# A twelve-phase decoder kernel: tree routing of all batches first, tile steps woven into the dense query chunks, five slot and sixteen weight buffers, and exponentials in halves

## The chip, the core and the metric

The kernel runs on one core of a Trainium2 chip. The core has TensorE (PE, matrix products and transposes), VectorE (DVE), ScalarE (ACT), GpSimd (POOL) and SyncE (SP). Each engine runs its own list of instructions in order, and they wait for each other through semaphores. The metric is the device time of one launch in microseconds, the lower the better. Tensors have 128 partitions; a matrix product writes PSUM banks of 512 float32 a partition.

## What is computed

x has 64 sequences of 64 tokens with 128 features. Twelve residual blocks run one after the other, each on the layer norm of x. Two kinds matter here. The first is softmax attention with 8 or 16 heads, in five of the blocks. The second is the third block, a memory attention whose queries, keys and values each come from a hard tree of experts:

```python
def _fff(x, node_w, node_b, w1, b1, w2, b2):
    cur = jnp.zeros((N,), jnp.int32)
    for _ in range(DEPTH):                      # DEPTH = 4: 15 nodes, 16 leaves
        pw = node_w[cur]
        score = jnp.einsum('nd,nd->n', xf, pw) + node_b[cur]
        cur = 2 * cur + 1 + (score >= 0).astype(jnp.int32)
    leaf = cur - N_NODES
    sel = jax.nn.one_hot(leaf, N_LEAVES, dtype=xf.dtype)
    hidden_all = jax.nn.relu(jnp.einsum('nd,ldh->lnh', xf, w1) + b1[:, None, :])
    hidden = hidden_all * sel.T[:, :, None]     # leaf width 64
    out = jnp.einsum('lnh,lho->no', hidden, w2) + sel @ b2

q, k, v = _fff(x, q_...), _fff(x, k_...), _fff(x, v_...)
x = x + softmax(q @ k.T / sqrt(128)) @ v        # inside each sequence of 64 tokens
```

## The kernel before

decoder() runs twelve phases with a barrier between them. x stays on chip. Phase 2 is trees(); phases 0, 3, 7, 9 and 10 are attention().

**trees().** The 4096 tokens are 32 tiles (NT), or 8 groups (g) of 512, or 4 batches (b) of 1024 for the routing. The names P = 128, GT = 4, NG = 8, NC = 8 run through it.

Routing of a batch: norm and shift_mean on DVE and root on POOL give the layer norm's factors. normalize on ACT writes xn. turn_x and take_x transpose it, score_nodes (PE) multiplies with the 45 nodes of the three trees, and decide, levels and count (DVE) make one-hot leaves and counts. turn_leaves (PE) and take_leaves (ACT) transpose the query leaves into selT; negate makes selneg of it. place (PE) and take_places (DVE) give each token its place among those of its leaf. After the fourth batch lay_tiles and give_slots turn places into slots, so that tokens of one leaf fill whole tiles of 128 rows. POOL scatters xn by slot into DRAM, once for the keys (r = 0) and once for the values (r = 1), 32 indirect DMAs each.

The queries are computed densely: for each group and each of 8 chunks of two leaves (m = 0..63), make_hidden(m + 1) multiplies, adds -1e30 to what the token's leaf doesn't hold, relu (ACT) follows, and add_leaf(m) adds up. A group ends with take_q. The order on PE is written out by hand: in front are batches 0 and 1, and batches 2 and 3 are routed inside the chunk loop, with turn_leaves and place at m = 4, 10 and 16.

Keys and values are computed by slot: each region r has 47 tiles (NTL) in 12 steps (NQ) of four. A step m is turn_rows (PE transposes four slots tiles), take_rows (DVE copy), hide_rows (PE), relu_rows (ACT), yield_rows (PE), take_results (DVE) and store_rows (SP). SP loads slots (load_slots, buffers RXS = 3) and a weight block for each tile (load_weights, RW_ = 12 buffers), each weight load behind a read of its row number from table. Steps of r = 0 are woven into the chunks from m = 48 (K_FROM), those of r = 1 run behind the last chunk, with the attention's first pieces between them.

The attention of a group: POOL gathers keys (got_k) and values (got_v, all eight groups in a row, after the last store), turn_k, score, shift, exps, turn_weights, take_weights, weigh (weights times values) and update (x += ...). weigh and update of all eight groups stand behind everything else. PSUM banks are H (two), Y, PJ, SC, XT, HS, YS.

**attention().** 32 tiles i of two sequences each. On PE, in this order: score(i + 1), turn(i), weigh(i), with projections of coming groups between. DVE takes the maximum and subtracts it (shift); ACT takes one exponential of 128x1024 (exps, line 689); turn(i) waits for it and transposes it in two halves of four products into TP, ACT copies each half to pT (take_turned), and weigh(i) multiplies with the values.

## Time and profile before

| | us |
|---|---|
| median of three runs | 2553.05 |
| the runs | 2552.4, 2553.05, 2559.71 |
| the profiled execution | 2557.27 |
| its span in the trace | 2555.3 |
| in it: trees(), from its first to its last instruction | 406.1 to 819.0 |
| in it: TensorE busy | 1864.2 (73%) |
| in it: VectorE, ScalarE, GpSimd busy | 1314.5, 1093.2, 745.8 |

All times in the trace count from the span's start. In its rows stands first when an instruction or a merged run of like instructions begins, then how long it lasts; in brackets how long its engine was idle before it, and which instruction or DMA ended that. SPq is SyncE's issuing of a DMA. Granted clock 1.00 is 2.4 GHz of TensorE and 0.50 is 1.2 GHz.

### The profile page before, as it was taken

How to read it: one execution, taken by the hardware profiler on the slowest of the kernel's cores; microseconds unless marked ns; L12 is line 12 of the kernel's file. 1: busy time of each engine (PE TensorE's matmuls, PEld its weight loads, DVE VectorE, ACT ScalarE, POOL GpSimd, SP SyncE). 2: the span in 40 equal slices, each digit the busy share in tenths (PEclk: the TensorE clock that was granted, in tenths of full speed). 3: DMA queues.
4: the chain of work that ended last, by engine and by line, in shares of the span. 5: the costliest groups of instructions: out<-in, count | busy, mean ns of one | idle time of the engine just before them, and what ended most of it. 6: DMA issues, size and time to landing. Idle time of an engine off the chain costs nothing. (4 is left out here: it accounts for less than half of the span.)

```text
span 2555.3 us, 39295 instructions
## 1 busy us (share of the span) xinstructions
PE 1864.2 (73%) x14689; PEld 1299.7 (51%) x14689; DVE 1314.5 (51%) x3517; ACT 1093.2 (43%) x2105; POOL 745.8 (29%) x625
## 2 busy tenths in 40 slices
PE   3876305897764897978999485997788868862895
PEld 1544203334453465766798353665545535552674
DVE  3887595201122675454343363775278847761223
ACT  3664402332221675843344243773346536630331
POOL 1232101272225321116455001321212122227353
PEclk9888756899655898877999586998879869965897
DMA  4111320024442500001476200000000000001224
GB/s 147 82 82 83 87 79 4 1 82 116 126 108 67 202 2 19 17 13 50 130 235 198 68 1 13 14 10 9 3 1 2 1 13 14 10 23 57 67 79 135
DMA packets 140655, 156.38 MB, mean 61 GB/s; under 512 B 19889, under 2 KB 126065, under 8 KB 139537
## 3 DMA queue, kind: packets, MB, share of 16 engines
q1 hardware_dynamic: 126644, 122.79, 15.5%
q0 software_dynamic: 13248, 28.21, 3.3%
q10 hardware_dynamic: 576, 2.88, 0.3%
q8 instruction: 118, 1.93, 0.3%
q14 instruction: 69, 0.57, 0.1%
HBM read 120.54 MB, written 68.57 MB: 74 GB/s over the span
## 5 line engine op out<-in xcount | busy, mean ns | idle before, releaser
L2696 POOL DMA_INDIRECT f_back<-f_ys,f_row x158 | 151.2, 957 | 177.8 <-DVE f_ys L2857 148.6
L836 PE MATMUL a_AV<-a_vx,a_pT 128*64 128x18 f32 (+1 forms) x3072 | 115.1, 223 | 48.9 <-DVE a_att L529 31.6
L836 PEld LDWEIGHTS a_AV<-a_vx,a_pT 128*64 128x64 f32 x3072 | 105.8, 146 | 79.3 <-issue 32.3
L2689 POOL DMA_INDIRECT f_slots<-f_pay,f_slot x128 | 124.2, 971 | 66.0 <-issue 38.2
L536 DVE TENSOR_REDUCE a_mx<-a_S 128x16 f32<-128x1024 f32 x96 | 117.5, 1224 | 41.0 <-PE a_S L812 39.0
L823 PE MATMUL a_TP<-ident,a_e 128*128 128x128 f32 x768 | 112.6, 295 | 32.7 <-ACT a_e L689 32.2
L823 PEld LDWEIGHTS a_TP<-ident,a_e 128*128 128x128 f32 x768 | 95.9, 152 | 65.6 <-ACT a_e L689 55.4
L689 ACT ACTIVATE a_e<-a_e 128x1024 f32<-128x1024 f32 x96 | 101.3, 1055 | 65.4 <-DVE a_e L539 65.4
L694 ACT COPY a_pT<-a_TP 128x512 f32<-128x512 f32 x192 | 104.1, 589 | 58.2 <-PE a_TP L823 58.0
L812 PE MATMUL a_S<-a_kbd,a_qT 64*64 64x512 f32 x768 | 118.0, 691 | 0.1
L539 DVE TENSOR_TENSOR a_e<-a_S,a_mx 128x1024 f32<-128x1024 f32 x96 | 117.1, 1219 | 1.9
L536 DVE TENSOR_REDUCE x_mx<-x_S 128x16 f32<-128x1024 f32 x64 | 78.4, 1225 | 51.7 <-PE x_S L812 51.2
L2923 ACT ACTIVATE f_h<-f_H,f_wt 128x256 f32<-128x256 f32 x156 | 67.0, 474 | 81.9 <-PE f_H L3019 81.9
L1465 DVE COPY f_xsT<-f_XT 128x512 f32<-128x512 f32 (+1 forms) x24 | 16.3, 681 | 157.3 <-PE f_XT L1697 157.3
L2923 ACT ACTIVATE f_h<-f_H,f_b 128x512 f32<-128x512 f32 (+1 forms) x96 | 58.0, 616 | 83.9 <-PE f_H L3019 83.9
L836 PE MATMUL x_AV<-x_vx,x_pT 128*64 128x18 f32 x2048 | 75.4, 217 | 20.8 <-DVE x_att L529 13.6
L836 PEld LDWEIGHTS x_AV<-x_vx,x_pT 128*64 128x64 f32 x2048 | 69.4, 144 | 40.6 <-issue 23.4
L386 POOL TENSOR_TENSOR x_kbd<-x_kT,x_mask 128x2048 f32<-128x2048 f32 x16 | 57.6, 3600 | 101.9 <-ACT x_kT L666 101.9
L694 ACT COPY x_pT<-x_TP 128x512 f32<-128x512 f32 x128 | 69.2, 589 | 40.1 <-PE x_TP L823 40.1
L674 ACT ACTIVATE a_kbd<-a_kT,a_mask 128x512 f32<-128x512 f32 x128 | 85.6, 723 | 0.4
L823 PE MATMUL x_TP<-ident,x_e 128*128 128x128 f32 x512 | 73.5, 290 | 15.9 <-ACT x_e L689 15.5
L386 POOL TENSOR_TENSOR a_kbd<-a_kT,a_mask 128x2048 f32<-128x2048 f32 x16 | 57.6, 3600 | 90.2 <-ACT a_kT L666 90.2
(478 smaller groups left out, 4724.4 us busy)
## 6 DMA issues: line engine op xcount, KB each, us to landing
f_wt<-in_f_ew SPq DMA_DIRECT2D x39, 584.0 KB
f_slots<-in_blank SPq DMA_DIRECT2D x1, 18576.0 KB
f_wt<-in_f_leaf SPq DMA_DIRECT2D x94, 98.0 KB, 2.0
f_pay<-f_back SPq DMA_DIRECT2D x8, 1024.0 KB, 8.2
f_xs<-f_slots SPq DMA_DIRECT2D x47, 144.0 KB
f_slots<-in_blank SPq DMA_DIRECT2D x1, 5760.0 KB
f_xs<-leaf_slots SPq DMA_DIRECT2D x22, 256.0 KB, 3.0
leaf_out<-f_ys SPq DMA_DIRECT2D x22, 256.0 KB, 2.2
```

Of the source, the lines that this page charges most:

```text
L386: pool.tensor_tensor(kbd[:, n % 2, :, 0:4, :], bc(kT[:, :].rearrange("p (b j) -> p b j", j=SL), 2, shape), mask8[:, 0:4].unsqueeze(1).unsq ...
L536: return v.tensor_reduce(mx[:, i % 2, :], unit(i), AX.X, ALU.max)
L539: v.tensor_tensor(e[:, i % 2, :, :], unit(i), bc(mx[:, i % 2, :], 2, [P, NH, SL]), ALU.subtract).then_inc(shifted.sem, 1)
L674: last = act.activation(kbd[:, n % 2, :, h, :], kT[:, :].rearrange("p (b j) -> p b j", j=SL), ACT.Copy, scale=mask8[:, h:h + 1])
L689: act.activation(e[:, i % 2, :, :], e[:, i % 2, :, :], ACT.Exp).then_inc(weights.sem, 1)
L694: act.copy(pT[:, 4 * n:4 * n + 4, :], TP[:, n, :].rearrange("p (a b) -> p a b", a=4)).then_inc(pT_half.sem, 1)
L812: last = pe.matmul(S[64 * c:64 * c + 64, i % 2, r, :], qT[rows, g % 2, SL * b:SL * b + SL], kbd[rows, g % 2, b, :, :], start=True, stop=True)
L823: last = pe.transpose(TP[:, half, P * n:P * n + P], ev[:, 4 * half + n, :], k.ident[:, :])
L836: last = pe.matmul(AV[64 * c:64 * c + 64, 2 * hp * W1:2 * (hp + 1) * W1], pT[:, hp, 64 * c:64 * c + 64], vx[:, g % 2, t, c, 2 * hp:2 * hp ...
L2689: pool.indirect_dma_start(out=slots[:, :], out_offset=bass.IndirectOffsetOnAxis(ap=slot[:, c, t:t + 1], axis=0), in_=pay[:, c, t, :], in_o ...
L2696: pool.indirect_dma_start(out=back[:, :], out_offset=bass.IndirectOffsetOnAxis(ap=row[:, i % RR, t:t + 1], axis=0), in_=ys[:, i % RY, t, : ...
L2923: act.activation(h[:, i % 2, c, 0:P * n], hid(i, c, n), ACT.Gelu_apprx_tanh, bias=weights(i)[2][:, c:c + 1])\
```

## The change

In trees(): all four batches are routed before the first chunk. On PE place(b - 1) comes behind score_nodes(b), and only turn_leaves(0) stays in front; the other three stand at chunks 8, 14 and 20. negate moves from POOL to DVE. All 24 tile steps stand in the chunk loop, from chunk 23 on (step i = m - 23). Key transposes, scores, weight transposes and value products of the eight groups follow at steps that four tables set (keys_at, scores_at, weights_at, values_at), in and behind the last chunks. Slots get five buffers and weights sixteen, and SP loads them five and four steps ahead of the step whose results it stores. Weights are transposed into HS instead of Y, and the value products go to XT and YS instead of PJ and XT. In attention() the exponential of a tile is two instructions of 128x512, and each half of turn(i) waits for its own.

```diff
@@ attention()
-    scores, shifted, weights = ph.counter("scores"), ph.counter("shifted"), ph.counter("weights")
+    scores, shifted, weights = ph.counter("scores"), ph.counter("shifted"), ph.counter("weights", 2)
...
-                act.activation(e[:, i % 2, :, :], e[:, i % 2, :, :], ACT.Exp).then_inc(weights.sem, 1)
+                for half in range(2):
+                    eh = e[:, i % 2, 8 * half:8 * half + 8, :]
+                    act.activation(eh, eh, ACT.Exp).then_inc(weights.sem, 1)
...
             def turn(i):
-                pe.wait_ge(weights.sem, weights.after(i))
                 for half in range(2):
+                    pe.wait_ge(weights.sem, 2 * i + half + 1)
@@ trees()
-    RW_, RXS = 12, 3
+    RW_, RXS = 16, 5
...
-    K_FROM = 48
+    NM = NG * NC
+    ROWS_FROM = 23
+    LAST = NM - ROWS_FROM + 5
+    leaves_at = {8: 1, 14: 2, 20: 3}
+    keys_at = {max(16 + 2 * g, 8 * g - 15): g for g in range(NG)}
+    scores_at = {25 + 2 * g if g < NG - 1 else 42: g for g in range(NG)}
+    weights_at = {27 + 2 * g if g < NG - 1 else 44: g for g in range(NG)}
+    values_at = {31 + 2 * g: g for g in range(NG)}
+    rows_at = lambda m: 0 <= m < 2 * NQ
...
@@ sync
-            for n in range(8):
-                load_weights(n)
-            for r in range(2):
-                sp.wait_ge(scattered[r].sem, scattered[r].after(NT - 1))
-                load_slots(r, 0)
-                load_slots(r, 1)
-                for j in range(NQ):
-                    if j + 2 < NQ:
-                        load_slots(r, j + 2)
-                    for n in range(NTL * r + 4 * j + 8, min(NTL * r + 4 * j + 12, NTL * r + NTL + 8, 2 * NTL)):
+            for m in range(4):
+                for n in tiles_of(m):
+                    load_weights(n)
+            sp.wait_ge(scattered[0].sem, scattered[0].after(NT - 1))
+            for m in range(RXS):
+                load_slots(m)
+            for m in range(2 * NQ):
+                store_rows(m)
+                if m + RXS == NQ:
+                    sp.wait_ge(scattered[1].sem, scattered[1].after(NT - 1))
+                if rows_at(m + RXS):
+                    load_slots(m + RXS)
+                if rows_at(m + 4):
+                    for n in tiles_of(m + 4):
                         load_weights(n)
-                    store_rows(r, j)
@@ gpsimd
-            root(0)
-            root(1)
             for b in range(NBAT):
-                negate(2 * b)
-                negate(2 * b + 1)
-                if b + 2 < NBAT:
-                    root(b + 2)
+                root(b)
@@ vector
             for b in range(NBAT):
                 decide(b)
                 levels(b)
                 count(b)
-                if b + 2 < NBAT:
-                    norm(b + 2)
-                    shift_mean(b + 2)
-                take_places(b)
+                if b:
+                    take_places(b - 1)
+            negate(0)
+            negate(1)
+            take_places(NBAT - 1)
             lay_tiles()
...
+            for g in range(2, NG):
+                negate(g)
             v.wait_ge(cleared.sem, 1)
-            for i in range(2 * NG + 3):
...
-            for g in range(NG):
-                update(g)
+            for i in range(LAST + 2):
+                if rows_at(i):
+                    take_rows(i)
+                if rows_at(i - 2):
+                    take_results(i - 2)
+                if i in scores_at:
+                    shift(scores_at[i])
+                if i in weights_at:
+                    add_weights(weights_at[i])
+                if i - 1 in values_at:
+                    update(values_at[i - 1])
@@ tensor
             make_hidden(0)
-            for m in range(NG * NC):
...
+            for m in range(LAST + ROWS_FROM + 1):
+                i = m - ROWS_FROM
+                if m + 1 < NM:
                     make_hidden(m + 1)
+                if m in leaves_at:
+                    turn_leaves(leaves_at[m])
+                if m < NM:
+                    add_leaf(m)
+                if rows_at(i):
+                    turn_rows(i)
+                if rows_at(i - 1):
+                    hide_rows(i - 1)
+                if rows_at(i - 2):
+                    yield_rows(i - 2)
+                if i in keys_at:
+                    turn_k(keys_at[i])
+                if i in scores_at:
+                    score(scores_at[i])
+                if i in weights_at:
+                    turn_weights(weights_at[i])
+                if i in values_at:
+                    weigh(values_at[i])
```

ScalarE's loop runs over the same m with relu(m + 1), take_leaves, take_q, relu_rows(i - 1), take_k, exps one step behind scores_at, and take_weights.

Two places show what moved. The first is VectorE between the counts of one batch and the decisions of the next. Before (f_nmr and f_var are layer norm's, f_places the copy of take_places, f_sc the node scores):

```order
L1422 TENSOR_TENSOR f_before<-f_before,f_cnt 128x256
L1382 BN_STATS f_stats<-x 128x6 x8
L1385 BN_AGGR f_mv<-f_stats 128x2 x8
L1387 TENSOR_SCALAR f_var<-f_mv 128x8
L1391 SCALAR_TENSOR_TENSOR f_nmr<-f_mv,f_rstd 128x8
L1426 COPY f_places<-f_YS 128x256
L1395 TENSOR_TENSOR f_sc<-f_SC,f_nodeb 128x360
```

And after, at the end of the last batch, with the first two negations in front of the last copy of places:

```order
L1423 TENSOR_TENSOR f_before<-f_before,f_cnt 128x256
L1427 COPY f_places<-f_YS 128x256
L1463 TENSOR_SCALAR f_selneg<-moe 32x512 x2
L1427 COPY f_places<-f_YS 128x256
L1431 COPY f_total<-f_SC 128x32
```

The norms have left the batch loop for its front, and the copy of a batch's places stands one batch later.

The second place is TensorE in a tile step of r = 1. Before, between two steps (f_XT, f_HS, f_YS are the step's three products, f_SC the scores, f_PJ the key transposes):

```order
L1740 MATMUL f_SC<-moe 64x64 x8
L1697 MATMUL f_XT<-ident,f_xs 128x128 x4
L1708 MATMUL f_HS<-f_xsT,f_wt 64x128 x4
L1720 MATMUL f_YS<-f_wt,f_hs 128x128 x4
L1728 MATMUL f_PJ<-ident,f_got_k 128x128 x4
```

After, a tile step of r = 1 in a dense chunk, and behind it the start of the next chunk:

```order
L1666 MATMUL f_H<-f0w 128x512
L1667 MATMUL f_H<-f_selneg,f_leaf 128x512
L1676 MATMUL f_Y<-f_h,f0w 128x512
L1687 MATMUL f_XT<-ident,f_xs 128x128 x4
L1696 MATMUL f_HS<-f_xsT,f_wt 64x128 x4
L1706 MATMUL f_YS<-f_wt,f_hs 128x128 x4
L1714 MATMUL f_PJ<-ident,f_got_k 128x128 x4
L1666 MATMUL f_H<-f0w 128x512
```

Each step of r = 1 has a dense chunk in front of it, and scores come only after the last step.

## Rows read from the trace of the kernel before

**Rows 1.** Stretches of the tree stage; the header row names the columns.
```profile
core 0: us, PE busy (x) PEld busy (x) DVE busy (x) ACT busy (x) POOL busy (x), PEclk, DMA share, GB/s
405.00:439.00 34.00, 15.04 (x73) 12.43 (x74) 17.86 (x95) 13.52 (x31) 11.73 (x11) 0.61 0.04 8
439.00:475.00 36.00, 26.95 (x81) 11.38 (x79) 5.20 (x27) 10.60 (x20) 5.46 (x3) 0.75 0.00 0
475.00:582.00 107.00, 107.00 (x285) 39.93 (x285) 17.64 (x40) 34.24 (x53) 62.53 (x60) 1.00 0.17 53
582.00:662.00 80.00, 64.52 (x299) 35.85 (x299) 15.64 (x23) 21.47 (x62) 7.80 (x9) 0.96 0.46 124
662.00:781.00 119.00, 78.78 (x433) 64.25 (x433) 28.88 (x56) 30.89 (x82) 35.24 (x38) 0.58 0.40 109
```

**Rows 2.** Timeline of routing and scatter: start us, us, engine, line, operation, idle before.
```profile
417.84 0.58 ACT L1545 COPY f0w<-f_PJ 128x512 f32<-128x512 f32 x1 [1.27 <-PE f_PJ L1634]
418.48 3.64 PE L1642 MATMUL f_SC<-f_nodes,f0w 128*128 128x45 f32 x16 [0.67 <-ACT f0w L1545]
422.26 0.53 DVE L1395 TENSOR_TENSOR f_sc<-f_SC,f_nodeb 128x360 f32<-128x360 f32 x1 [9.21 <-PE f_SC L1642]
424.89 0.58 ACT L1545 COPY f0w<-f_PJ 128x512 f32<-128x512 f32 x1 [1.27 <-PE f_PJ L1634]
425.42 1.04 PE L1651 MATMUL f_XT<-ident,f_selq 128*32 128x128 f32 x4 [0.57 <-DVE f_selq L1416]
426.02 0.43 DVE L1422 TENSOR_TENSOR f_before<-f_before,f_cnt 128x256 bf16<-128x256 bf16 x1
...
428.11 0.38 PE L1662 MATMUL f_YS<-f_before,f_ones 128*128 128x256 bf16 x1
439.06 1.91 PE L1675 MATMUL f_H<-f0w 128*128 128x512 f32 x2
445.45 1.02 PE L1675 MATMUL f_H<-f0w 128*128 128x512 f32 x2
...
503.35 0.42 DVE L1426 COPY f_places<-f_YS 128x256 f32<-128x256 f32 x1 [10.30 <-PE f_YS L1662]
510.41 1.90 POOL L1355 DMA_INDIRECT leaf_slots<-f_xn,f_slot  x1 [3.50 <-DVE f_slot L1445]
553.12 1.53 SPq L1303 DMA_DIRECT2D f_xs<-leaf_slots  x3
```

**Rows 3.** Timeline of one woven tile step, TensorE and SyncE's issues.
```profile
597.62 0.38 SPq L1309 DMA_DIRECT2D leaf_out<-f_ys  x1
598.05 0.51 SPq L1303 DMA_DIRECT2D f_xs<-leaf_slots  x1
599.66 3.70 SPq L1296 DMA_DIRECT2D f_wt<-in_f_leaf  x4
601.13 0.66 PE L1697 MATMUL f_XT<-ident,f_xs 128*128 128x128 f32 x4 [2.03 <-DMA f_xs<-leaf_slots]
...
603.72 1.02 PE L1675 MATMUL f_H<-f0w 128*128 128x512 f32 x2
604.64 0.38 SPq L1309 DMA_DIRECT2D leaf_out<-f_ys  x1
605.00 1.13 PE L1685 MATMUL f_Y<-f_h,f0w 128*128 128x512 f32 x2
```

**Rows 4.** Timeline: the bias product that stands in front of every eighth chunk.
```profile
540.78 1.02 PE L1683 MATMUL f_Y<-moe,f_b 32*128 32x512 f32 x2
```

**Rows 5.** Scores at full clock, value gathers (page group), last update.
```profile
775.89 0.69 PE L1740 MATMUL f_SC<-moe 128*64 128x64 f32 x16 [0.95 <-DVE f_e L1480]
...
L1371 POOL DMA_INDIRECT f_xn<-leaf_out,f_slot x32 | 30.2, 943 | 15.1 <-issue 15.1
...
817.88 1.12 DVE L1493 SCALAR_TENSOR_TENSOR x<-f_XT,f_rs,x 128x128 f32<-128x128 f32 x4 [3.78 <-PE f_XT L1758]
```

**Rows 6.** Exponentials, grouped: count | busy us, mean ns | idle before.
```profile
L689 ACT ACTIVATE a_e<-a_e 128x1024 f32<-128x1024 f32 x96 | 101.3, 1055 | 65.4 <-DVE a_e L539 65.4
L1993 ACT ACTIVATE x_ebd<-x_e 64x512 f32<-64x512 f32 x16 | 10.1, 629 | 0.1
```

**Rows 7.** Line 689: who waited for the exponential, us and times.
```profile
  PE a_TP L823: 32.2, 19
  PE x_TP L823: 15.5, 17
```

More of the change, by code:

```diff
@@ L1762, in _ @@
             pe.wait_ge(k.f0_in, 32)
[L1763 to L1772 removed]
+            for b in range(NBAT):
+                turn_x(2 * b)
+                turn_x(2 * b + 1)
+                score_nodes(b)
+                if b:
+                    place(b - 1)
+                if b == 1:
+                    turn_leaves(0)
```

208 lines of the change are left out of this document (66 added, 142 removed).

## The prediction

> **What bounds the kernel now.** I read the page's span first, then the stretches of the tree stage, then that stage's timelines, and last the rows of the attentions. The diff touches two places: trees(), which runs once, and the exponential of attention(), 160 times in five attentions.
>
> The tree stage runs from 405 us to 819.0 us, where its last update of x ends [rows 5]: 414 of 2555.3 us. It has four parts, limited by different things [rows 1]. From 405 to 475 us batches are routed one behind the other and TensorE is little busy at half clock. From 475 to 582 TensorE is busy in 107.0 of 107 us at granted clock 1.00: dense query chunks, and nothing can go faster there. From 582 to 662 twelve tile steps are woven into chunks, and each waits for its slots. From 662 to 781 the other twelve tile steps run bare, at clock 0.58. Then value gathers run alone on GpSimd to the end. So about 190 us of the stage have TensorE waiting or at half clock, while the work that it waits for could lie under the dense chunks.
>
> Why the woven steps wait is in one step [rows 3]: SyncE stores step results at 597.62, issues the slots at 598.05, and TensorE's transpose starts at 601.13, 3.1 us later, after 2.03 us idle. The next slots are issued behind a store that needs the step before; the cycle takes 604.64 - 597.62 = 7.02 us. TensorE's own work in it is 603.72 - 601.13 = 2.59 us for the tile step (transposes, hidden, results) and one dense chunk, 605.00 - 603.72 = 1.28 and 0.96 for its last two products: 2.23. Together 4.8 us.
>
> **Routing.** After the change all four batches are routed before the first chunk. A batch takes 424.89 - 417.84 = 7.05 us between its last copies [rows 2]. Batch 1 ends at 425.5 as before. In front of each later batch TensorE now has place() too, and once turn_leaves(0); both together take 428.49 - 425.42 = 3.1 us, place() alone some 1.8 with its hand-overs. So batch 2 ends at 425.5 + 7.05 + 3.1 = 435.7, batch 3 at 435.7 + 7.05 + 1.8 = 444.5. Node scores take 3.64 us, and VectorE from scores to counts 426.45 - 422.26 = 4.2 us [rows 2]: 452.5. Then come take_places(2) and the two negations that the change moves from GpSimd to VectorE. These are not seen on VectorE: between 0.42 us (its 256-column pass at 503.35) and 0.84 (twice that) each; I take 0.6, since one pass has 512 columns but a part of its time is fixed. The last place() runs beside them (1.8) and is what ends last: the last take_places starts at 454.9. Before, that copy stood at 503.35 and the first scatter came 7.06 us later at 510.41 [rows 2]. After: 454.9 + 7.1 = 462.0, **48.4 us earlier**. The first chunk moves the other way, from 439.06 to about 455.2. GpSimd has no tensor work left behind which a scatter could queue.
>
> **Start of the woven part.** Slots can be read 553.12 - 510.41 = 42.7 us after the first scatter: at 504.7, landed at 507.8. Chunk 23, where tile step 0 stands, starts at 455.2 + 6.4 (the first two chunks at half clock, 439.06 to 445.45 [rows 2]) + 22 x 2.23 + 2 x 0.95 (bias product [rows 4]) + 2.6 (three pairs of leaf transposes, 0.9 each at full clock) = 515.2. No wait there; the second region's scatter ends 40 us after the first, near 545, and its slots are first wanted by SyncE near 568: none there either.
>
> **Woven part: SyncE sets the pace.** Slots are now five steps ahead and weights four, so the 3.1 us of a slot load are hidden. But SyncE's own queue per step is a store, a slot load and four weight loads with a row number each: 597.62 to 599.66 + 3.70 = 603.36, 5.75 us [rows 3]. That is more than TensorE's 4.8. The first store is possible after step 2. Step 0 has only transposes (2.8 with its chunk), step 1 no results (3.8), step 2 is whole (4.8), and the copy for the store ends 0.9 later: 515.2 + 12.3 = 527.5. Its lead of about 4 us over TensorE is used up after four to five more steps; from then on a step costs 5.75 us. The last weights (step 23) are issued 19 rounds later: 527.5 + 19 x 5.75 - 1.1 (one round has three tiles) + 6.3 (store, slot load and three weights, and 2.0 to landing) = 642. TensorE alone would have come to its hidden product of step 23 at 515.2 + 23.7 (to that of step 4) + 19 x 4.8 + 4.6 (bias products, key transposes) = 634.7. So I count **642**: 24 tile steps with 24 chunks take 127 us, where before 24 tile steps with 14 chunks took the 199 us from 582 to 781.
>
> **The remaining chunks and the attention of the trees.** Behind it are 15 full chunks and a last half: 34.4; two bias products 1.9; and, as pieces between the chunks, the last results and key transposes (1.7 + 2.3), seven score products at 0.69 [rows 5] (4.8), seven weight transposes at 0.45 (3.2), five value products at about 1.0 (5.0). The transposes and value products are an estimate from the tile step's 2.59 us, which is four transposes, the cheapest, and twice four products. That makes 642 + 53.3 = 695.3. The tail that no chunk covers (last keys, scores, exponential, transpose, value product, update, with hand-overs) is 9.5 us: 704.8. GpSimd's value gathers do not set this end: 32 at 0.943 + 0.30 us [rows 5], begun after the key gathers at 655.5, end at 695.5 and land 2.5 later; the last value product wants them near 702. That cover is only 4 us: if TensorE ran 4 us ahead of my sum, the gathers would be late next.
>
> Sum: 704.8 - 819.0 = -114.2. For hand-overs inside 16 mixed chunks and one table load of the exponential (1.3 us) I give 2 us back: **-112 us**. The ends: -122 if SyncE keeps to TensorE's pace (-7.3) and routing runs partly at full clock (-3); -98 if TensorE drops to half clock for some 30 us in it (+14).
>
> **Exponential in halves.** The exponential of 128x1024 takes 1055 ns [rows 6]. A 512-column one from SBUF takes 629 ns [rows 6], so the first half is ready 0.43 us sooner, and the second 0.10 to 0.20 us later than now (two of 629 ns are 1258, if they don't overlap). TensorE's four transposes of the first half take about as long as the four at 601.13, 0.66 us [rows 3], so they cover the delay. The gain lies only where TensorE stands idle for the exponential: 36 times, 47.7 us in all [rows 7], mostly long waits of which only 0.43 can go; 36 x 0.43 = 15.5 is the ceiling. What is late next on many of these tiles is VectorE (its take_values frees AV) or the copies of pT, so I take a bit under half: **-6 us**, between -14 and +5. The plus end is ScalarE's extra time where it is the late one: 0.20 us in 25 of 160 tiles.
>
> The Trainium skill (ScalarE: Activation LUTs, What ACT_TABLE_LOAD costs) gives an ACTIVATE a fixed part of 186 ns and 0.833 ns a column, with 93 ns overlap behind another. That is 1039 ns for the whole, where the trace shows 1055, and 1132 for two halves. By it the second half would be 0.09 us late instead of 0.10 to 0.20. The Trainium skill (Advanced Engine Details and Errata, The Read-Write Bubble) also speaks against the edit, since it advises tiles of 512 or 1024 elements to keep such bubbles few. If the whole fixed part were on the path of every tile, 160 x 0.093 = 15 us would come on top, and the sum would be -97 instead of -118.
>
> **Sum.** -112 - 6 = -118 us. The profiled execution took 2557.27 us round a span of 2555.3; the median of the three runs is 2553.05, 4.2 lower. I take the difference off the median: **2435 us**.
>
> **Rivals.**
> A: the tile steps are not held by SyncE but by TensorE (weight loads overlap better than their issue rows say): step 4.8 us, seven us less, of which the value gathers take back some three. 2431 us. For it: rows of idle SyncE before each round. Against: 3.70 us for four issues is measured with nothing to wait for.
>
> B: the clock. TensorE was at 1.00 in 475 to 582 and 0.96 in the woven part, and 0.58 where tile steps ran bare [rows 1]. If woven steps paced by SyncE (TensorE wanted for 4.8 of 5.75 us) let it fall for longer, chunk and step go from 4.8 to about 9 us; for a third of the steps that is 8 x (9 - 5.75) = 26 us. 2461 us. Against: before, steps of 7.02 us with 2 us idle kept the clock.
>
> C: ScalarE is what the attentions wait for. Two activations instead of one cost 0.20 us more in each of 160 tiles: +32 us instead of -6. 2473 us. Against: it waits 65.4 us before the exponentials of a_ tiles alone [rows 6], longer than all the extra time.
>
> D: slower than before. The chain store, slot load, weights, step is not opened by the deeper buffers, because everything still runs in one SyncE queue behind a store that waits for results; at half clock a round of bare steps took about 9.3 us (12 steps in 662 to 781 with the rest between [rows 1]). It ends above 2553 only from 5.75 + 118 / 24 = 10.7 us a step on; at 11 us it would be 24 x 5.25 = 126 us more, 2561 us. Against: nothing in five-deep slots asks for the step before.
>
> E: the change does less than it says: routing first ends later (DVE, ACT and PE hand over at half clock) and the scatter moves only 25 us; then step 0 waits about 15 us at chunk 23 and everything behind shifts. 2450 us.
>
> **How the numbers follow.** My forecast (SyncE-paced) 0.60; A 0.12; B 0.10; C 0.04; D 0.02; E 0.12. The terms' ends give 2553 - 122 - 14 = 2417 to 2553 - 98 + 5 = 2460. The range of 8 in 10 takes in forecast, A, E and the near side of B: **2419 to 2458**. A measurement of this kernel can tell about 0.3%, 8 us, from no change; all cases but D lie far below that: faster 0.97, same 0.01, slower 0.02.
>
> **What would show it.** In the changed kernel's profile: first scatter near 462 us; first slots near 505; from about the ninth woven step TensorE waits for weights, stores 5.75 us apart; clock 1.00 from about 465 to 700; no stretch of value gathers alone; stage end near 705. In the attentions, shorter waits of the transposes on the exponential, and tile periods shorter by some 0.04 us. The prediction is wrong if step 0 waits for slots, if TensorE's clock falls in the woven part, or if the attentions grow longer.

## The result, and the profile after

The changed kernel takes 2440.22 us (median of four runs, 2427.66 to 2448.57) where the kernel before, run beside it, takes 2554.95: a ratio of 0.9552, 95% interval 0.9529 to 0.9575. The forecast was 2435, in 2419 to 2458. The profiled execution of the changed kernel is the longest of the four, 2448.57 us round a span of 2446.6. In it the tree stage begins 6.15 us later than in the trace of before (of the phases ahead of it attention a0, where the diff changes only the exponential, and warping, which it leaves alone, took 3.1 us more each), so 6.15 is taken off its times below where they are compared with the forecast.

From first to last instruction, in the two profiled executions:

| stage | before, us | after, us | difference |
|---|---|---|---|
| tree stage | 412.9 | 299.6 | -113.3 |
| attention a0 | 242.6 | 245.7 | +3.1 |
| attention a1 | 181.3 | 181.2 | -0.1 |
| attention x2 | 185.5 | 184.3 | -1.2 |
| attentions a3 and x3 | 427.4 | 430.2 | +2.8 |
| warping, not touched | 142.0 | 145.1 | +3.1 |
| routed, not touched | 292.8 | 295.7 | +2.9 |
| pooling, not touched | 141.8 | 137.9 | -3.9 |

The tree stage is as much shorter as was forecast. The five attentions together are 4.5 us longer here (1037.0 to 1041.5), where the forecast had them 6 shorter. Stages that the diff does not touch move by as much as the attentions do, so one pair of traces says nothing on the exponential; that took runs.

The stretches of the tree stage in the changed kernel, to be read beside [rows 1] (columns as there):

```profile
412.00:460.00 48.00, 29.49 (x142) 25.08 (x143) 27.86 (x139) 18.06 (x42) 9.81 (x10) 0.51 0.03 6
460.00:520.00 60.00, 60.00 (x149) 21.26 (x149) 14.43 (x29) 20.48 (x32) 40.85 (x41) 0.97 0.32 93
520.00:648.00 128.00, 118.19 (x585) 67.80 (x583) 30.70 (x45) 45.02 (x118) 44.00 (x47) 1.00 0.60 162
648.00:712.00 64.00, 61.08 (x355) 32.43 (x354) 23.41 (x67) 28.90 (x55) 38.47 (x41) 1.00 0.25 65
```

Routing (first line) still runs at about half clock. Behind it TensorE is busy in 239 of 252 us at granted clock 0.97 to 1.00. The long stretch at 0.58 of [rows 1] is gone. What is left over is 9.8 us of idle TensorE in the third line, where the tile steps are woven in.

The ends of routing and scatter, and the last update, in the timeline (start us, us, engine, line, operation, idle before), to be read beside [rows 2, 5]:

```profile
457.77 0.42 DVE L1427 COPY f_places<-f_YS 128x256 f32<-128x256 f32 x1
458.11 0.74 DVE L1463 TENSOR_SCALAR f_selneg<-moe 32x512 bf16<-32x512 f32 x2
459.71 0.42 DVE L1427 COPY f_places<-f_YS 128x256 f32<-128x256 f32 x1 [0.86 <-PE f_YS L1653]
...
466.76 1.87 POOL L1358 DMA_INDIRECT leaf_slots<-f_xn,f_slot  x1 [42.56 <-DVE f_slot L1446]
...
710.68 1.12 DVE L1498 SCALAR_TENSOR_TENSOR x<-f_YS,f_rs,x 128x128 f32<-128x128 f32 x4 [0.68 <-PE f_YS L1749]
```

The first scatter stands at 466.76 - 6.15 = 460.6 (forecast 462.0; before 510.41 [rows 2]). The last update ends at 711.80 - 6.15 = 705.65 (forecast 704.8; before 819.0 [rows 5]).

One woven tile step, to be read beside [rows 3]:

```profile
592.34 0.43 SPq L1318 DMA_DIRECT2D leaf_out<-f_ys  x1
...
592.82 0.51 SPq L1312 DMA_DIRECT2D f_xs<-leaf_slots  x1
...
593.94 0.43 PE L1696 MATMUL f_HS<-f_xsT,f_wt 128*64 128x128 f32 x2 [0.73 <-DMA f_wt<-in_f_leaf]
...
594.38 3.72 SPq L1305 DMA_DIRECT2D f_wt<-in_f_leaf  x4
...
597.53 0.60 PE L1687 MATMUL f_XT<-ident,f_xs 128*128 128x128 f32 x4
...
598.14 0.43 SPq L1318 DMA_DIRECT2D leaf_out<-f_ys  x1
...
599.76 0.43 PE L1696 MATMUL f_HS<-f_xsT,f_wt 128*64 128x128 f32 x2 [0.73 <-DMA f_wt<-in_f_leaf]
```

The transposes at 597.53 no longer wait for slots. What waits is the hidden product, inside its run of eight, for the weights of the tiles that SyncE issued last. SyncE's stores stand 598.14 - 592.34 = 5.80 us apart and it issues without a pause: in these rows it sets the pace. Not every round is that short. The 19 rounds that the forecast counts, from the first store at 532.81, take 113.2 us, 5.96 each. The view of TensorE's waits over the woven stretch names nothing else of size:

```profile
PE f_HS L1696 <- DMA f_wt<-in_f_leaf: 8.1, 12, 1.2
PE f_PJ L1714 <- DMA f_got_k<-leaf_out,f_slot: 1.6, 1, 1.6
```

In the attentions, the costliest groups of the page (count | busy us, mean ns | idle before, and who ended it), beside [rows 6, 7]:

```profile
L838 PE MATMUL a_AV<-a_vx,a_pT 128*64 128x18 f32 (+1 forms) x3072 | 116.1, 224 | 58.5 <-DVE a_att L529 38.4
...
L691 ACT ACTIVATE a_e<-a_e 128x512 f32<-128x512 f32 x192 | 110.1, 622 | 74.7 <-DVE a_e L539 74.6
...
L825 PE MATMUL a_TP<-ident,a_e 128*128 128x128 f32 x768 | 116.1, 300 | 26.2 <-ACT a_e L691 26.0
```

TensorE's idle time for the exponential fell from 32.2 [rows 7] to 26.0 us, as forecast. But on the line of the value products 58.5 us of idle time stand, and in the kernel before that group and the transposes have these rows:

```profile
L836 PE MATMUL a_AV<-a_vx,a_pT 128*64 128x18 f32 (+1 forms) x3072 | 115.1, 223 | 48.9 <-DVE a_att L529 31.6
...
L823 PE MATMUL a_TP<-ident,a_e 128*128 128x128 f32 x768 | 112.6, 295 | 32.7 <-ACT a_e L689 32.2
```

What was won ahead of the transposes seems to be waited again a step later, for VectorE. The first experiments test that.

### The profile page after: what moved, and what is told of

It reads as the page before. It is cut to its first block and busy times, and to the rows that moved or that the text cites. A ratio compares the mean times of both kernels' runs of the same rounds, so it can differ in the third digit from the quotient of the medians.

```text
span 2446.6 us, 39610 instructions
## 1 busy us (share of the span) xinstructions
PE 1829.2 (75%) x14689; PEld 1272.8 (52%) x14689; DVE 1326.4 (54%) x3525; ACT 1110.3 (45%) x2265; POOL 731.0 (30%) x617
## 5 line engine op out<-in xcount | busy, mean ns | idle before, releaser
L838 PE MATMUL a_AV<-a_vx,a_pT 128*64 128x18 f32 (+1 forms) x3072 | 116.1, 224 | 58.5 <-DVE a_att L529 38.4
L691 ACT ACTIVATE a_e<-a_e 128x512 f32<-128x512 f32 x192 | 110.1, 622 | 74.7 <-DVE a_e L539 74.6
L825 PE MATMUL a_TP<-ident,a_e 128*128 128x128 f32 x768 | 116.1, 300 | 26.2 <-ACT a_e L691 26.0
L2894 ACT ACTIVATE f_h<-f_H,f_wt 128x256 f32<-128x256 f32 x156 | 66.7, 474 | 81.6 <-PE f_H L2990 81.6
L838 PE MATMUL x_AV<-x_vx,x_pT 128*64 128x18 f32 x2048 | 75.0, 216 | 23.8 <-DVE x_att L529 16.6
L838 PEld LDWEIGHTS x_AV<-x_vx,x_pT 128*64 128x64 f32 x2048 | 69.0, 144 | 43.6 <-issue 23.8
L386 POOL TENSOR_TENSOR x_kbd<-x_kT,x_mask 128x2048 f32<-128x2048 f32 x16 | 57.6, 3600 | 101.4 <-ACT x_kT L666 101.4
L1559 ACT ACTIVATE f_h<-f_H,f_b 128x512 f32<-128x512 f32 x64 | 44.0, 687 | 89.1 <-PE f_H L1667 89.1
L386 POOL TENSOR_TENSOR a_kbd<-a_kT,a_mask 128x2048 f32<-128x2048 f32 x16 | 57.6, 3600 | 88.9 <-ACT a_kT L666 88.9
L378 POOL TENSOR_TENSOR a_rstd<-a_var,neghalf 128x4 f32<-128x4 f32 x24 | 24.3, 1014 | 199.2 <-DVE a_var L449 112.2
```

Of the source, the lines that this page charges most:

```text
L386: pool.tensor_tensor(kbd[:, n % 2, :, 0:4, :], bc(kT[:, :].rearrange("p (b j) -> p b j", j=SL), 2, shape), mask8[:, 0:4].unsqueeze(1).unsq ...
L691: act.activation(eh, eh, ACT.Exp).then_inc(weights.sem, 1)
L825: last = pe.transpose(TP[:, half, P * n:P * n + P], ev[:, 4 * half + n, :], k.ident[:, :])
L838: last = pe.matmul(AV[64 * c:64 * c + 64, 2 * hp * W1:2 * (hp + 1) * W1], pT[:, hp, 64 * c:64 * c + 64], vx[:, g % 2, t, c, 2 * hp:2 * hp ...
L2894: act.activation(h[:, i % 2, c, 0:P * n], hid(i, c, n), ACT.Gelu_apprx_tanh, bias=weights(i)[2][:, c:c + 1])\
```

## Experiments

Three sets of four kernels, each set on one chip with the kernel before beside it. In the third set the kernel before itself took 2654.0 us and no longer 2553 to 2554 as in the first two; what the traces show of it is in the last section. Ratios are always to the kernel before of the same set.

### The exponential alone

Only the three hunks of attention() on the kernel before:

```
+                for half in range(2):
+                    eh = e[:, i % 2, 8 * half:8 * half + 8, :]
+                    act.activation(eh, eh, ACT.Exp).then_inc(weights.sem, 1)
...
                 for half in range(2):
+                    pe.wait_ge(weights.sem, 2 * i + half + 1)
```

> The kernel before, with only the exponential of the attentions in two halves. H1 (my forecast): the first half is ready 0.43 us sooner and the gain lies where TensorE stands idle for it: 6 us less than before, 2549 us. H2 (nothing left of it): in the changed kernel's profile the waits of the transposes on the exponential are shorter, but value products wait longer for VectorE's copy instead (a_AV idle 48.9 to 58.5 us), and the five attentions together are 4.5 us longer in that one execution: within 3 us of before. H3 (ScalarE bound): 10 us or more above before.

Measured: 2553.97 us (12 runs) against 2553.11 (23 runs), ratio 1.0000, interval 0.9978 to 1.0021. The forecast's -6 us (0.9977) lies just outside it; a gain of more than 5.6 us is excluded at that level. The time is that of H2.

The price of the second instruction without the early first half: as above, but the transposes wait for both.

```
+                for half in range(2):
+                    eh = e[:, i % 2, 8 * half:8 * half + 8, :]
+                    act.activation(eh, eh, ACT.Exp).then_inc(weights.sem, 1)
...
                 pe.wait_ge(weights.sem, weights.after(i))
                 for half in range(2):
```

> The kernel before with two half exponentials, but TensorE's transposes still wait for both: the price of the second instruction without what the early first half gives. If the second half ends 0.1 to 0.2 us later than one whole exponential and that is on the path only in the 36 tiles whose transposes stood idle for it, 4 to 7 us above before; if ScalarE is the bound in every tile, 160 x 0.2 = 32 us above before. The difference to the kernel with halves and no such wait is what the early first half gives: H1 10 to 13 us, H2 under 5 us.

Measured: 2563.75 us, ratio 1.0033, interval 1.0015 to 1.0052, that is +8.4 us (3.8 to 13.3), a bit above the 4 to 7 expected, though the interval holds these too. The two kernels with halves stand 2563.75 - 2553.97 = 9.8 us apart by their medians and 8.4 by their ratios: that is what the early start of the first half is worth once there are two instructions. It is near the 10 to 13 of H1 and not under 5 as in H2, so the two expectations point different ways; against the kernel before, which is what counts, nothing is gained. The groups of the page show where it goes. Of the kernel with halves:

```profile
L838 PE MATMUL a_AV<-a_vx,a_pT 128*64 128x18 f32 (+1 forms) x3072 | 114.9, 223 | 57.6 <-DVE a_att L529 37.3
...
L825 PE MATMUL a_TP<-ident,a_e 128*128 128x128 f32 x768 | 111.7, 292 | 25.7 <-ACT a_e L691 25.5
```

Of the kernel with halves that waits for both:

```profile
L838 PE MATMUL a_AV<-a_vx,a_pT 128*64 128x18 f32 (+1 forms) x3072 | 115.6, 224 | 53.7 <-DVE a_att L529 36.1
...
L825 PE MATMUL a_TP<-ident,a_e 128*128 128x128 f32 x768 | 112.9, 295 | 35.3 <-ACT a_e L691 35.2
```

Idle time of TensorE ahead of transposes and value products together, in the a_ tiles: before 32.7 + 48.9 = 81.6 us; halves 25.7 + 57.6 = 83.3; halves with the wait 35.3 + 53.7 = 89.0. From before to halves 7.0 us go at the first and 8.7 come back at the second. The x_ tiles, by the same groups, do alike: before 15.9 + 20.8, halves 8.8 + 24.6, with the wait 17.2 + 18.6. In all, 14.1 us less in front of the transposes and 12.5 more in front of the value products, most of it waiting for VectorE. The changed kernel's trace has nearly the same (26.2 + 8.6 and 58.5 + 23.8).

The later second half is not what TensorE waits for in the kernel with halves. It stands idle for an exponential 23 times there, each time ahead of a tile's first transpose, never ahead of the fifth, which is the one that needs the second half. In the kernel that waits for both, every such wait (45) is for the second half.

### The tree stage alone, and the changed kernel again

The changed kernel with these lines of attention() as before:

```
-                for half in range(2):
-                    eh = e[:, i % 2, 8 * half:8 * half + 8, :]
-                    act.activation(eh, eh, ACT.Exp).then_inc(weights.sem, 1)
+                act.activation(e[:, i % 2, :, :], e[:, i % 2, :, :], ACT.Exp).then_inc(weights.sem, 1)
```

> The changed kernel with the exponential of the attentions whole again, so only the tree stage is changed. The tree stage took 113.3 us less in the changed kernel's trace. With H1 this kernel is 112 us under before and 6 above the changed one: 2443 us. With H2 it is the same as the changed kernel, 114 under before. With H3 it is 10 us or more faster than the changed kernel.

Measured: 2441.88 us, ratio 0.9570, interval 0.9545 to 0.9594; tree stage 295.8 us. No edit, the changed kernel once more:

> The changed kernel once more, beside the others on the same chip. Its four first runs lay between 2427.7 and 2448.6 us. If that spread belongs to the kernel (a race between SyncE and TensorE in the woven part that falls out differently), its tree stage is of another length in another execution; if it belongs to the chip, the tree stage stays within 1 us of 299.6 and the attentions differ. Median 2436 to 2444 us.

Measured: 2434.98 us, ratio 0.9531, interval 0.9507 to 0.9556; tree stage 296.0 us. The kernel with whole exponentials is 6.9 us slower than this one by the medians, which is what H1 said, and the two intervals overlap only from 0.9545 to 0.9556. But the trace of the kernel with whole exponentials has the shorter attentions (the five together 1033.9 us, where the changed kernel's two traces have 1041.5 and 1037.0), and the intervals of it and of the changed kernel's first four runs (0.9529 to 0.9575) do overlap in most of their length. So the tree stage carries the gain; on the changed kernel an exponential worth some 6 us is neither shown nor excluded by these runs. The pair on the kernel before, with 12 and 23 runs, is the closer test. The second statement of the expectation fell: the tree stage was not within 1 us of 299.6 but 3.6 shorter. The nine runs of the changed kernel have a median of 2435.5 us and lie between 2427.7 and 2448.6. The 3.6 us are not in the woven steps (first to last transpose 123.9 and 123.3 us) nor behind them (66.0 in both), but ahead of step 0, which comes 109.7 and 106.7 us behind the start of the stage; TensorE's granted clock from 412 to 460 us is 0.51 in the one trace and 0.57 in the other. So the spread of the changed kernel is not a race of SyncE and TensorE in the woven part; stages that the diff does not touch vary too (routed 295.7 and 290.7).

### Is it SyncE that sets the pace of the woven steps?

Weights from fixed rows, so that SyncE reads no row number (the tiles get other leaves' weights):

```
-                at = sp.value_load(table[0:1, r, i:i + 1], min_val=0, max_val=(2 * LV - 1) * P)
-                sp.dma_start(wt[:, n % RW_, :], d["f0_leaf"][bass.ds(at, P), :]).then_inc(wt_in[n % RW_].sem, 16)
+                sp.dma_start(wt[:, n % RW_, :], d["f0_leaf"][P * (n // 3):P * (n // 3) + P, :]).then_inc(wt_in[n % RW_].sem, 16)
```

> The changed kernel, but the tile steps load their weights from fixed rows: SyncE reads no row number ahead of a load. It leaves out that each tile gets the weights of its own leaf (rows of tree weights are chosen by number n // 3 instead). P1 (my forecast: SyncE's queue sets the pace of the woven part): a round falls from 5.8 us to about 4 x 0.43 + 2 x 0.43 = 2.6, below TensorE's 4.8; stores come 4.8 us apart, TensorE no longer waits for weights, the tree stage is 5 to 9 us shorter than 296 to 300, the kernel 2427 to 2433 us. P2 (TensorE sets the pace, rival A): under 2 us shorter.

Measured: 2415.07 us, ratio 0.9462, interval 0.9425 to 0.9498; tree stage 282.6 us, 13.4 less than the 296.0 of the changed kernel. SyncE in one round of it:

```profile
578.25 0.49 SPq L1311 DMA_DIRECT2D f_xs<-leaf_slots  x1
578.78 1.97 SPq L1304 DMA_DIRECT2D f_wt<-in_f_leaf  x4
582.74 0.38 SPq L1317 DMA_DIRECT2D leaf_out<-f_ys  x1
```

Four weight loads take 1.97 us instead of 3.72, they begin 0.04 us behind the slot load and not 1.05 (594.38 - 592.82 - 0.51 in the changed kernel's rows above), and then SyncE waits 2 us for the next result. A row number read costs SyncE so (3.72 - 1.97 + 1.05 - 0.04) / 4 = 0.69 us, 2.8 a round. In the changed kernel's trace such a read is a load of 0.26 to 0.28 us (0.56 behind a slot load), register operations of 0.15 and 0.04 and a check of the bounds (0.02), with short pauses between them; the timeline leaves these out. P1, and the gain is larger than its 5 to 9 us: from the first to the last transpose of the 24 steps it is 110.6 us instead of 123.3 in the changed kernel's second trace, and TensorE is not idle once from 460 to 648 us.

The other direction, every row number read twice:

```
                 at = sp.value_load(table[0:1, r, i:i + 1], min_val=0, max_val=(2 * LV - 1) * P)
+                at = sp.value_load(table[0:1, r, i:i + 1], min_val=0, max_val=(2 * LV - 1) * P)
```

> The changed kernel with each row number read twice by SyncE. A read takes 0.26 us behind another read and 0.62 behind a load, so a round grows by 4 x 0.26 = 1.0 us to 4 x 0.6 = 2.4 us. P1: all of it is on the path for 19 rounds: the tree stage 19 to 45 us longer, 2457 to 2483 us, stores 6.8 to 8.2 us apart. P2: less than half of that, since TensorE had room of 1 us a step.

Measured: 2469.93 us, ratio 0.9688, interval 0.9647 to 0.9730; tree stage 341.2 us, 45.2 longer, the upper end of P1. Of these 38.5 lie in the 24 steps (161.8 us from first to last transpose), 2.9 ahead of step 0, where the changed kernel's own two traces differ by as much, and 3.9 behind the steps. A round is now

```profile
578.45 0.43 SPq L1319 DMA_DIRECT2D leaf_out<-f_ys  x1
578.93 0.51 SPq L1313 DMA_DIRECT2D f_xs<-leaf_slots  x1
581.11 5.67 SPq L1306 DMA_DIRECT2D f_wt<-in_f_leaf  x4
586.83 0.43 SPq L1319 DMA_DIRECT2D leaf_out<-f_ys  x1
```

586.83 - 578.45 = 8.38 us, 2.6 more than 5.80; times 19 rounds that would be 49 us. Not all rounds are that long: the 19 take 153.2 us where the changed kernel has 113.2, 40.0 more. TensorE's clock is no longer kept either, which the stretch of the woven steps shows (columns as in [rows 1]):

```profile
520.00:648.00 128.00, 108.21 (x451) 58.52 (x449) 23.92 (x35) 34.65 (x93) 31.54 (x35) 0.87 0.46 123
```

That is rival B at a round of 8.4 us; at 5.8 us the same stretch has 1.00. The fall of the clock adds little to what the longer rounds cost: SyncE waits for results no longer than in the changed kernel (27.0 and 27.5 us in all, 20 of them for the first), so it is still SyncE that is late.

### What the deeper slot buffers do

```
-    RW_, RXS = 16, 5
+    RW_, RXS = 16, 3
```

> The changed kernel with three slot buffers again, so a slot load is issued three steps ahead and not five. Before, with two steps ahead, a step took 7.02 us: store, slot load, 3.1 us to TensorE's transpose. With three ahead the slots asked for behind the store of step m are wanted by step m + 3, which is the step after the next one: if two steps of 4.8 us (9.6) cover the 3.1 us, nothing changes (within 3 us of the changed kernel) and of the deeper buffers only the third step was needed. If depth five is what removes the wait, 24 x (7.0 - 5.8) = 29 us are lost, 2469 us. I expect the first, at 0.6.

Measured: 2492.91 us, ratio 0.9787, interval 0.9736 to 0.9838; tree stage 349.8 us. My expectation was wrong: more than the whole 29 us of the second case were lost, 53.8, of which 49.1 in the 24 steps (172.4 us from first to last transpose for 123.3). The timeline shows why:

```profile
577.67 0.38 SPq L1318 DMA_DIRECT2D leaf_out<-f_ys  x1
...
578.10 0.51 SPq L1312 DMA_DIRECT2D f_xs<-leaf_slots  x1
...
581.17 0.66 PE L1687 MATMUL f_XT<-ident,f_xs 128*128 128x128 f32 x4 [1.17 <-DMA f_xs<-leaf_slots]
```

The transposes wait for the very slot load that was issued 3.07 us before. It is [rows 3] again. Of TensorE's waits from 520 to 700 us the view has one line:

```profile
PE f_XT L1687 <- DMA f_xs<-leaf_slots: 32.2, 19, 2.7
```

These 32.2 us are not the whole 49.1: the granted clock of the stretch from 520 to 648 us is 0.85 here, where five buffers have 1.00. A load three steps ahead of the step whose store it follows is no load ahead at all, since that store comes two steps late. I had counted from the step that owns the store, not from the step that is running.

With four buffers there is one step between:

```
-    RW_, RXS = 16, 5
+    RW_, RXS = 16, 4
```

> The changed kernel with four slot buffers. With three, steps stood 7.0 to 9.0 us apart and the tree stage took 350 us instead of 296: slots of step m + 3 are issued behind the store of step m, and that store can only go after the third step behind m has begun, so nothing is asked for ahead. S1 (only the place of the issue behind the store counts): with four there is one whole step (4.8 us) between the issue and the use, more than the 3.1 us of before, so the kernel is the same as the changed one, tree stage 296 to 300, 2435 to 2441 us. S2 (each step of depth gives its share): half of the loss of three, tree stage near 322, 2465 us.

Measured, in the third set: 2562.05 us, ratio 0.9654, interval 0.9627 to 0.9682, beside 0.9531 and 0.9552 for the changed kernel in other sets (the last section says why ratios of this set can't be compared with those). The 24 steps take 132.3 us from the first to the last transpose, where five buffers take 123.3 and three 172.4. So the first extra step gives 40 us and the second 9: nearer to S1, but not all of it. About 1 of the 9 may belong to the set, since the kernel of the next section has 111.7 us in this set and 110.6 in the second. The transposes still wait for slots 15 times in the 24 steps, where five buffers leave no such wait:

```profile
PE f_XT L1687 <- DMA f_xs<-leaf_slots: 16.5, 15, 2.5
```

### Stores and slot loads off SyncE's queue

SyncE keeps only the weight loads. ScalarE issues the store of step i - 3 and, behind the relu of step i - 1, the slots:

```
+                if rows_at(i - 3):
+                    store_rows(act, i - 3)
                 if rows_at(i - 1):
                     relu_rows(i - 1)
+                    if rows_at(i - 1 + RXS):
+                        if i - 1 + RXS == NQ:
+                            act.wait_ge(scattered[1].sem, scattered[1].after(NT - 1))
+                        load_slots(act, i - 1 + RXS)
```

> The changed kernel with the stores and the slot loads of the tile steps issued from ScalarE's queue, and only the weight loads left on SyncE. SyncE's round is then 4 x 1.12 = 4.5 us, under TensorE's 4.8; ScalarE issues two transfers more a step (0.8 us) beside about 2 us of work in 4.8. P1: stores 4.8 to 5.0 us apart, the tree stage 5 to 9 us shorter than 296 to 300, unless the 32 value gathers on GpSimd, which already ended 6 us before the stage did, then hold the end: 2427 to 2433 us. P2: within 2 us of the changed kernel. If ScalarE's waits for results ahead of its own work block it: slower.

Measured: 2424.6 us, ratio 0.9501, interval 0.9470 to 0.9531; tree stage 283.9 us, 12.1 less than 296.0. It is the fastest kernel here that computes everything, though its interval overlaps those of the changed kernel (0.9507 to 0.9556 and 0.9529 to 0.9575, in other sets); that it is faster rests on the stage. Its 24 steps take 110.6 us, the same as with fixed weight rows: two ways to relieve SyncE end at the same pace, TensorE's. They stand 4.55 to 4.78 us apart wherever no bias product or key transpose lies between, and the woven stretch has no idle time:

```profile
520.00:648.00 128.00, 128.00 (x667) 75.96 (x667) 34.39 (x53) 53.98 (x137) 49.17 (x52) 1.00 0.65 175
```

The same with three slot buffers:

> The kernel with stores and slot loads on ScalarE's queue, with three slot buffers. There the slot load of step m + 3 stands behind the relu of step m and not behind its store, so it is issued two steps ahead of its use. S1 (the issue's place behind the store was the wait, not the number of buffers): steps stay at 4.8 us, the tree stage at 284, 2421 to 2428 us, where three buffers on SyncE's queue took 2493. S2 (the buffers themselves): the steps go to 7 us and more, 2470 us or above.

Measured, in the third set: 2541.01 us, ratio 0.9592, interval 0.9561 to 0.9623; the 24 steps take 111.7 us where five buffers took 110.6, at the same 4.78. S1 in the steps: not the number of buffers made the wait but where in the queue the load stands. The time of the whole, 2421 to 2428, did not come, because of what disturbs the third set; within the set the ratio is below that of four buffers on SyncE's queue (0.9654), in the order expected.

### Without the cover of the dense chunks

```
-    ROWS_FROM = 23
-    LAST = NM - ROWS_FROM + 5
+    ROWS_FROM = 48
+    LAST = 46
```

> The changed kernel with routing first, depth five and four, but the tile steps begin at chunk 48 as before and not at chunk 23: what the first and the third part are worth without the cover of dense chunks. Step 0 comes 25 chunks later, at about 575 us; 16 steps lie in chunks at 5.3 to 5.75 us, eight are bare, at SyncE's 5.75 us a step if the clock does not matter to it or up to 9.3 us as the bare steps of before; then gathers, scores and value products run bare as before (some 50 us). The tree stage takes 345 to 370 us: 45 to 70 us less than before, and 50 to 75 more than the changed kernel, 2485 to 2510 us. The granted clock falls to the half level in that last part.

Measured, in the third set: 2603.44 us, ratio 0.9831, interval 0.9797 to 0.9865: 51 us less than before and 41 us more than the kernel with four buffers beside it. Stretches (columns as in [rows 1]): woven steps, bare steps, the rest.

```profile
640.00:700.00 60.00, 58.86 (x291) 34.33 (x290) 15.77 (x23) 21.48 (x59) 0.00 (x0) 0.97 0.50 132
700.00:770.00 70.00, 55.14 (x245) 38.55 (x243) 14.95 (x22) 16.06 (x50) 20.80 (x22) 0.68 0.61 158
770.00:853.00 83.00, 31.53 (x269) 26.11 (x268) 23.00 (x67) 16.92 (x36) 39.63 (x42) 0.63 0.19 51
```

The clock holds while steps are woven in chunks and falls to 0.68 and 0.63 once they are bare, as in [rows 1]. Queue, buffers and routing give 51 of the 92 us that the kernel with four buffers gains beside it (the 51 lie inside the expected 45 to 70), the cover of the chunks the other 41. This kernel has five slot buffers, though, and its neighbour four, which cost that one some 9 us in its steps; so the cover is worth about 41 + 9 = 50 us as an estimate from these runs, the lower end of the expected 50 to 75. The 24 steps are hardly longer without it (127.1 us from first to last transpose): what is lost is the work that the chunks hid, not the pace of the steps. How it divides without the disturbance of this set stays open. No run has the early routing alone or the deeper weight buffers alone, so what each of these is worth is not shown.

### The first hidden product in the hole of routing

On the kernel with ScalarE's queue:

```
-            negate(0)
-            negate(1)
+                if b == NBAT - 2:
+                    negate(0)
+                    negate(1)
...
+            make_hidden(0)
             place(NBAT - 1)
             count_all()
-            make_hidden(0)
```

> The kernel with stores and slot loads on ScalarE's queue, and also the first hidden product put into TensorE's 3.5 us hole ahead of the last place(), with the two negations ahead of the last batch. Since TensorE was busy without a gap from 455 us to the end of the chunks there, its 2.65 us at half clock go and VectorE's 0.74 too: the tree stage 2.5 to 3.5 us shorter than 283.8, first scatter 0.5 to 0.8 us earlier. In whole runs that is 0.1%, which cannot be told from 2424.6 us; against before the ratio should be near 0.949.

Measured, in the third set: 2547.24 us, ratio 0.9591, interval 0.9563 to 0.9620, the same as its neighbour with three slot buffers (0.9592). The first scatter comes 52.9 us behind the start of the stage (462.41 - 409.55) where it came at 52.8 with ScalarE's queue and five buffers (460.61 - 407.83) and at 52.4 with three (461.22 - 408.80): no gain. The place() behind the product shows it:

```profile
453.98 0.37 PE L1652 MATMUL f_YS<-f_selkv,f_tri 128*128 128x256 bf16 x1 [1.28 <-DVE f_places L1422]
```

It still waits for VectorE's copy of places; the product filled 2.2 us of the hole, and the leaf transposes behind chunk 8 come 2.4 and 1.2 us earlier against the start of the stage than in these two. Whether that reaches the end can't be told from these runs.

## Why the prediction was right, point by point

- **Routing first.** Right. First scatter at 460.6 for 462.0. One term was on the high side: the two negations take 0.74 us together, not 1.2.
- **Start of the woven part.** Right. Step 0's transposes stand at 521.94 - 6.15 = 515.8 for 515.2 and wait for nothing; nothing waits for the second scatter either.
- **SyncE sets the pace.** Right, and shown from both sides: fewer reads make the stage 13.4 us shorter, twice the reads 45.2 longer, and other transfers on another queue 12.1 shorter. The first wait for weights stands in the ninth step. The shortest rounds take 5.80 us for 5.75, but the mean is 5.96: the 19 rounds took 113.2 us where the sum had 108.2. The last hidden product is at 651.28 - 6.15 = 645.1 for 642 and not 5 us late, since the first store came 0.8 us sooner than in the sum (532.81 - 6.15 = 526.7 for 527.5) and what follows the last round took 5.3 us and not 6.3.
- **Rival A** was refuted by the same runs, but its price was too low: a TensorE that nothing holds takes 110.6 us from first to last transpose, 12.7 less than 123.3, and the forecast had 7.3. From step 0's transposes to the last hidden product the sum had 119.5 us for TensorE alone, and both kernels that relieve SyncE take 115.4; SyncE's 126.8 was 129.3. So both sides were mis-sized. TensorE's steps are 4.78 us and some 4.55 for the 4.8, and the first steps, bias products and key transposes came cheaper than their terms.
- **Rival B** did not come: clock 0.97 to 1.00 from 460 to 712. It is real at longer rounds: 0.87 from 520 to 648 us with the doubled reads and 0.85 with three slot buffers.
- **Behind the woven part.** Right: 60.5 us from the last hidden product to the stage end for 62.8. Value gathers end at 699.7 for 695.5 (taken to the time of before), still no bound.
- **The exponential.** Wrong in size: -6 forecast, 0 measured (-5.6 to +5.4) on the kernel before. The step that failed is the share of the 15.5 us ceiling that stays, "a bit under half". Ahead of the transposes nearly the whole ceiling was won, 14.1 us of idle time in the trace of the kernel with halves; 12.5 of it came back ahead of the value products. The forecast named VectorE as what is late next and let it take half; it takes nearly all. That the four transposes of the first half cover the second half's delay held: none of the 23 waits is for the second half. The sign that the forecast itself gave, attentions that grow longer, came in one trace of the changed kernel (1041.5 us for 1037.0) and not in the other (1037.0); they are shorter in neither. The busy time of the exponential rose from 101.3 to 110.1 us over 96 tiles, 0.09 us each. The rule of the Trainium skill (ScalarE: Activation LUTs, What ACT_TABLE_LOAD costs) that made the second half 0.09 us late agrees with the trace's 0.09; the 15 us that it would cost if all of it were on the path are an upper bound, which even the kernel that waits for both halves does not reach with its 8.4. Two readings there were wrong: the -97 has the 15 us in place of the -6 (on top of the -118 it is -103), and the advice of the Trainium skill (Advanced Engine Details and Errata, The Read-Write Bubble) names tiles of 512 elements beside those of 1024, so it does not speak against this edit, whose halves have 512 columns each.
- **Rivals C, D, E** did not come. C's sign is right where the transposes wait for both halves: the second instruction then costs 8.4 us, a quarter of its 32. D's mechanism, a queue that is not opened by deeper buffers, is what three buffers have (7.0 to 9.0 us a step) and five do not.

Terms: tree stage -113.3 and, with the second trace, -116.9 for -112; exponential 0 for -6. That the whole came out 5 us from the forecast is in part luck: SyncE's rounds were 5.0 us longer than their term, the piece behind the woven part 2.3 shorter, and a tree stage somewhat better than its sum stands against an exponential that gave nothing.

## What to carry to other kernels

Count how far ahead a load is from the step that is running when the queue gets to it, not from the number of buffers: a load behind a store that is two steps late needs three buffers only to stand still, and moving it out of that queue made three buffers as good as five (111.7 and 110.6 us for the 24 steps). When a stage is paced by a queue, add up what the queue's own engine does per round; here reads of row numbers were 2.8 of 5.8 us, and another engine's idle queue took the transfers at no cost that the traces show. Splitting an instruction so that its first half is ready sooner pays only as far as what comes after the waiting engine is not late itself: here TensorE's idle time moved from its transposes to its value products, where VectorE holds it, 12.5 of 14.1 us.

## What was not expected of the hardware

In the third set every kernel, the one before too, took some 100 us longer (2654.0 for 2553). The waits view puts 146 to 158 us of idle time down to a releaser called remote in each of its four traces, mostly holes of 9 to 19 us on ScalarE (one of 38.5) and up to 32 us on VectorE in stretches in which GpSimd issues indirect transfers, and none in any of the ten earlier traces. The view of the kernel with ScalarE's queue and three slot buffers, from 460 to 560 us:

```profile
ACT f_h L1554 <- remote: 64.6, 6, 15.5
```

and its timeline of ScalarE with the first of these holes:

```profile
483.28 0.57 ACT L1550 COPY moe<-f_HS 32x512 f32<-32x512 f32 x1 [5.09 <-DMA moe<-dist_dram]
499.38 0.69 ACT L1554 ACTIVATE f_h<-f_H,f_b 128x512 f32<-128x512 f32 x1 [15.52 <-remote]
```

Its input, the hidden product of TensorE, had been finished since 483.15, for 16 us. The profile calls what ended the wait remote, so it is nothing that this core's instructions show, and I did not find the cause. TensorE's stretch round the hole has a lower granted clock too (columns as in [rows 1]): 31.54 of 60 us busy at 0.77, where the kernel with ScalarE's queue and five buffers, in the second set, is busy throughout at 1.00.

```profile
460.00:520.00 60.00, 31.54 (x68) 10.54 (x66) 7.65 (x15) 8.62 (x13) 45.06 (x46) 0.77 0.24 73
```

Steps outside the holes were as long as in the other sets (4.78 us). Whole times of this set are used only as ratios to the kernel before of the same set, and these ratios are not those of the other sets: the kernel with ScalarE's queue has 0.9592 here with three buffers and 0.9501 there with five, although its 24 steps take 111.7 and 110.6 us. By that difference (0.009 of 2553 us) the holes cost the changed kernels some 20 us more than the kernel before, an estimate; this set shows that much less of what a change gains.

A read of a row number by SyncE ahead of a transfer costs 0.69 us of its queue, more than the issue of the transfer itself (1.97 / 4 = 0.49).
